# Five stages of a perceiver layer begin with the products of the high rows, and two VectorE steps change places

## The reference

```python
x = x + _L0_xattn_ref(_layernorm(x, axis=-1), mask, ctx, ctx, wq, wk, wv, wo)
x = x + _L0_attn_ref(_layernorm(x, axis=-1), Wqa, g_qa, Wqb, Wkva, g_kva, Wkvb, Wo)
x = x + _L0_ffn_ref(_layernorm(x, axis=-1), router_w, router_bias, w_gate, w_up, w_down, sw_gate, sw_up, sw_down)

# in _L0_xattn_ref: q = x @ wq.T, k_new = x @ wk.T, v_new = x @ wv.T, softmax attention, out @ wo.T
# in _L0_attn_ref:
q_c = rms_norm(hidden_states @ Wqa, g_qa)
q = (q_c @ Wqb)                                  # 16 heads of 128 + 64, the 64 turned (rope)
kv = hidden_states @ Wkva
kv_exp = rms_norm(kv[..., :128], g_kva) @ Wkvb   # keys and values of the heads
# in _L0_ffn_ref: silu(x @ gate) * (x @ up) @ down for each expert, weighted by the router
```

## Time and profile before

| | |
|---|---|
| median of 3 runs | 521.59 us (520.97 to 521.95) |
| the profiled execution | 520.81 us |
| its span, first to last instruction | 519.0 us |
| PE busy | 509.2 us, 98% |
| DVE busy | 402.4 us, 78% |
| ACT busy | 301.6 us, 58% |
| POOL busy | 29.6 us, 6% |
| read from memory | 85.46 MB |

### The profile page before, as it was taken

One profiled execution on the slowest core, in us unless ns is written; L12 is line 12 of the kernel. 1 busy time (PEld: TensorE's weight loads), 2 busy tenths in 40 slices (PEclk: granted clock), 3 DMA queues, 4 the chain that ended last, 5 costly groups with the idle time before them and its releaser, 6 DMA issues.

```text
span 519.0 us, 10261 instructions
## 1 busy us (share of the span) xinstructions
PE 509.2 (98%) x3796; PEld 472.7 (91%) x3796; DVE 402.4 (78%) x627; ACT 301.6 (58%) x437; POOL 29.6 (6%) x49
## 2 busy tenths in 40 slices
PE   9999999999999999989999999999999999999997
PEld 7999999999778998869899999999999999999997
DVE  6776668997888888877797768677776777778675
ACT  5656556873367676665664564646555465655631
POOL 1000000000623113001000000000000000000000
DMA  8765553674412233424536565564646556565521
GB/s 285 302 206 190 170 164 94 191 202 138 152 37 78 77 125 118 130 114 156 211 122 218 159 229 169 197 194 170 228 154 225 174 189 207 165 231 157 210 71 40
DMA packets 19460, 86.25 MB, mean 166 GB/s; under 512 B 2160, under 2 KB 2416, under 8 KB 19312
## 3 DMA queue, kind: packets, MB, share of 16 engines
q1 hardware_dynamic: 19440, 85.99, 49.6%
HBM read 85.46 MB, written 0.52 MB: 166 GB/s over the span
## 4 chain that ended last, share of the span: by engine, by line
PE 81%; DVE 10%; ACT 3%; DMA 3%; issue 2%; SPq 1%; DVEq 0%; ACTq 0%
PE bank L1014 32%; PE bank L443 11%; PE bank L447 11%; PE bank L446 11%; PE bank L451 4%; PE bank L454 4%; PE bank L455 4%; DVE w_lo L296 3%; DMA raw<-ctx_t_dram 1%; DMA raw<-wk_dram 1%; ACT w_hi L291 1%; DVE score_rows L1418 1%; DVE operands L1423 1%; PE bank L792 1%; DVE operands L323 1%
## 5 line engine op out<-in xcount | busy, mean ns | idle before, releaser
L291 ACT CAST w_hi<-raw 128x768 fp32r<-128x768 f32 (+3 forms) x158 | 159.4, 1039 | 95.6 <-PE bank L1014 82.2
L296 DVE TENSOR_TENSOR w_lo<-raw,w_hi 128x1280 fp32r<-128x1280 f32 (+3 forms) x156 | 183.2, 1211 | 14.9 <-ACT w_hi L291 13.9
L1014 PE MATMUL bank<-xt_hi,w_hi 128*128 128x256 f32 x512 | 105.5, 277 | 0.2 <-DVE w_lo L296 0.2
L1014 PE MATMUL bank<-xt_hi,w_lo 128*128 128x256 f32 x512 | 105.4, 277 | 0.0
L1014 PE MATMUL bank<-xt_lo,w_hi 128*128 128x256 f32 x512 | 105.2, 277 | 0.0
L1014 PEld LDWEIGHTS bank<-xt_hi,w_hi 128*128 128x128 f32 x512 | 81.7, 188 | 3.3 <-DVE w_lo L296 0.6
L1014 PEld LDWEIGHTS bank<-xt_lo,w_hi 128*128 128x128 f32 x512 | 79.8, 188 | 0.0
L1014 PEld LDWEIGHTS bank<-xt_hi,w_lo 128*128 128x128 f32 x512 | 79.7, 188 | 0.0
L443 PE MATMUL bank<-w_hi,operands 128*128 128x512 f32 (+1 forms) x194 | 74.9, 386 | 1.0 <-DVE operands L344 1.0
L447 PE MATMUL bank<-w_hi,operands 128*128 128x512 f32 (+1 forms) x194 | 74.1, 382 | 0.0
L446 PE MATMUL bank<-w_lo,operands 128*128 128x512 f32 (+1 forms) x194 | 73.8, 380 | 0.0
(11 more groups left out here) (202 smaller groups left out, 865.4 us busy)
## 6 DMA issues: line engine op xcount, KB each, us to landing
raw<-w_exp_dram SPq DMA_DIRECT2D x34, 896.0 KB, 4.8
raw<-w_exp_dram SPq DMA_DIRECT2D x34, 640.0 KB, 5.6
raw<-ctx_t_dram SPq DMA_DIRECT2D x16, 512.0 KB, 4.4
raw<-ctx_n_dram SPq DMA_DIRECT2D x16, 512.0 KB, 4.0
raw<-w_mla_dram SPq DMA_DIRECT2D x8, 512.0 KB, 3.5
raw<-w_mla_dram SPq DMA_DIRECT2D x8, 448.0 KB, 3.7
raw<-wq_dram SPq DMA_DIRECT2D x4, 256.0 KB, 5.4
raw<-wk_dram SPq DMA_DIRECT2D x2, 512.0 KB, 7.2
```

The lines of the kernel that those rows point to most:

```text
L291: act.copy(w_hi[:, t.slot, at:at + n], raw[:, t.slot, at:at + n]).then_inc(hi_split[k], 1)
L296: eng.tensor_tensor(w_lo[:, t.slot, at:at + n], raw[:, t.slot, at:at + n], w_hi[:, t.slot, at:at + n].bitcast(F32), ALU.subtract) \
L1014: return pe.matmul(bank[b + u][:, m * T:m * T + T], a[:, t.slot, at + m * P:at + m * P + P], x[:, c, :], start=c == 0 and a is w_hi and x ...
```

## The change

At five places a wait for the low part moves behind the products that need only the high part.

- `project_q`: for the first chunk, the products of both weight parts with `xt_hi` come first, for all four column blocks, behind a wait on `ev_hi`; then the four with `xt_lo`, behind the wait on `ev_lo`. Two of the three products of zeros behind the second half's transposes are gone.
- `qkv_half`: a new function `token_rows` does the eight products with `xt_hi` of a half, then what stood `midway`, then the four with `xt_lo`.
- `rope_queries`: two products with `qc_hi`, then the wait, then the one with `qc_lo`.
- The first pair's keys: four products with `kvc_hi`, then the wait, then two with `kvc_lo`.
- `expert_rows` with `split`: the gate's products of each half by `token_rows`.

On DVE, `center(1)` moves ahead of the low parts of half 0. The arithmetic is the same but for the order of the sums in a bank.

```diff
@@ project_q
-                        pe.wait_ge(ev_lo, V_LN1 + 1 + c)
+                        pe.wait_ge(ev_hi if c == 0 else ev_lo, V_LN1 + 1 + c)
+                    if c == 0:
+                        for a, x in ((w_hi, xt_hi), (w_lo, xt_hi), (w_hi, xt_lo)):
+                            if x is xt_lo:
+                                pe.wait_ge(ev_lo, V_LN1 + 1)
+                            for m in range(NC):
+                                pe.matmul(bank[2 + m // 2][:, (m % 2) * T:(m % 2) * T + T],
+                                          a[:, 0, m * P:m * P + P], x[:, 0, :], start=False, stop=False)
+                        continue
...
-                for _ in range(1 + 2 * h):
-                    zeros(7, True)
+                zeros(7, True)
@@ qkv_half
+            def token_rows(o, h, moving, number, told=None, midway=None, first_half=None):
+
+                for c in range(NC):
+                    if c % 2 == 0:
+                        pe.wait_ge(ev_hi, number + c // 2)
+                    hi, lo = moving(c)
+                    ins = pe.matmul(o, xt_hi[:, c, half(h)], hi, start=c == 0, stop=False)
+                    if told is not None and c == 0:
+                        ins.then_inc(told, 1)
+                    pe.matmul(o, xt_hi[:, c, half(h)], lo, start=False, stop=False)
+                if midway is not None:
+                    midway()
+                for c in range(NC):
+                    if c % 2 == 0:
+                        pe.wait_ge(ev_lo, number + c // 2)
+                    ins = pe.matmul(o, xt_lo[:, c, half(h)], moving(c)[0], start=False, stop=c == NC - 1)
+                    if first_half is not None and c == 1:
+                        ins.then_inc(first_half, 1)
+                return ins
+
             def qkv_half(h, midway):
...
-                for c in range(NC):
-                    if c % 2 == 0:
-                        pe.wait_ge(ev_lo, V_LN2 + 2 * h + c // 2)
...
-                    if c == 2 - h:
-                        midway()
+                ins = token_rows(bank[2 + h][:, 0:384], h, columns, V_LN2 + 2 * h, midway=midway,
+                                 first_half=used[0] if h == 1 else None)
@@ rope_queries
-                product(bank[turned(h, g)][:, :], (qc_hi[:, 0, half(h)], qc_lo[:, 0, half(h)]),
-                        (rope_w[:, 0, g, :], rope_w[:, 1, g, :]), True, False, told)
+                pe.wait_ge(ev_hi, V_C + h)
+                ins = pe.matmul(bank[turned(h, g)][:, :], qc_hi[:, 0, half(h)], rope_w[:, 0, g, :],
+                                start=True, stop=False)
...
+                pe.matmul(bank[turned(h, g)][:, :], qc_hi[:, 0, half(h)], rope_w[:, 1, g, :], start=False, stop=False)
+                pe.wait_ge(ev_lo, V_C + h)
+                pe.matmul(bank[turned(h, g)][:, :], qc_lo[:, 0, half(h)], rope_w[:, 0, g, :], start=False, stop=False)
...
-            pe.wait_ge(ev_lo, V_C)
...
-            pe.wait_ge(ev_lo, V_C + 1)
@@ first pair of heads
+            pe.wait_ge(ev_hi, V_C + 3)
+            for hd in range(2):
+                for a in (w_hi, w_lo):
+                    pe.matmul(qk(hd)[:, T:2 * T], a[:, t.slot, 384 + hd * P:512 + hd * P], kvc_hi,
+                              start=False, stop=False, skip_group_check=True)
             pe.wait_ge(ev_lo, V_C + 3)
             for hd in range(2):
-                keys(t, hd)
+                pe.matmul(qk(hd)[:, T:2 * T], w_hi[:, t.slot, 384 + hd * P:512 + hd * P], kvc_lo,
+                          start=False, stop=True, skip_group_check=True).then_inc(bank_full[4 + 3 * hd], 1)
@@ expert_rows
+                    if u == 0 and split is not None:
+                        if h == 0:
+                            ready(t, 0)
+                        ins = token_rows(bank[b][:, 0:I], h, lambda c: wcols(t, c * I, I), split, told=told)
+                        continue
@@ VectorE
             add_attended(1)
+            center(1)
             tokens_lo(dve, 0, V_LN2, xt_hi, xt_lo, 0)
-            center(1)
             tokens_lo(dve, 4, V_LN2 + 2, xt_hi, xt_lo, 1)
```

More of the change, by code:

```diff
@@ L714, in transpose_kv, with columns @@
                 ins.then_inc(bank_full[5 + h], 1)
+            def token_rows(o, h, moving, number, told=None, midway=None, first_half=None):
[16 more added lines that the diff above has]
+                return ins
             def qkv_half(h, midway):
                 t = Tile(0, T_QKV)
-                for c in range(NC):
-                    if c % 2 == 0:
-                        pe.wait_ge(ev_lo, V_LN2 + 2 * h + c // 2)
[L721 to L726, removed]
-                    if c == 2 - h:
-                        midway()
+                def columns(c):
+                    return wcols(t, OFF[c // 2] + (c % 2) * 384, 384)
+                if h == 0:
+                    for k in range(2):
+                        ready(t, k)
+                ins = token_rows(bank[2 + h][:, 0:384], h, columns, V_LN2 + 2 * h, midway=midway,
+                                 first_half=used[0] if h == 1 else None)
                 ins.then_inc(bank_full[2 + h], 1)
@@ L738, in rope_queries @@
             def rope_queries(h, g, told=None):
-                product(bank[turned(h, g)][:, :], (qc_hi[:, 0, half(h)], qc_lo[:, 0, half(h)]),
-                        (rope_w[:, 0, g, :], rope_w[:, 1, g, :]), True, False, told)
+                pe.wait_ge(ev_hi, V_C + h)
+                ins = pe.matmul(bank[turned(h, g)][:, :], qc_hi[:, 0, half(h)], rope_w[:, 0, g, :],
+                                start=True, stop=False)
+                if told is not None:
+                    ins.then_inc(told, 1)
+                pe.matmul(bank[turned(h, g)][:, :], qc_hi[:, 0, half(h)], rope_w[:, 1, g, :], start=False, stop=False)
+                pe.wait_ge(ev_lo, V_C + h)
+                pe.matmul(bank[turned(h, g)][:, :], qc_lo[:, 0, half(h)], rope_w[:, 0, g, :], start=False, stop=False)
             def rope_queries_rest(g):
@@ L981, in expert_rows @@
                             ready(t, k)
-                        if split is not None and u == 0 and c % 2 == 0:
-                            pe.wait_ge(ev_lo, split + c // 2)
                         at = (u * NC + c) * I if k == 0 else OFF[2] + (c - 1) * I
```

## The result

The changed kernel took 518.43 us in the median of 18 executions (517.85 to 525.62), the kernel before 521.27 us in the median of 18 beside it (519.81 to 527.21): a ratio of 0.9944, 95% interval 0.9921 to 0.9966. The gain is 2.84 us where 1.65 us was forecast, and the time lies under the whole range of 518.9 to 520.9.

A forecast was written before the change was run, and what follows sets the result against it. TensorE's work plus its holes bound the kernel, so only holes could be won: 0.4 + 1.25 + 0 = 1.65 us off the profiled 520.81 gives 519.15, plus 0.78 to the median gives 519.9 us; range 518.9 to 520.9.

The forecast's parts named there:

- Place 1: First projection: first product at 8.33 instead of 8.78, shift 0.45 us, of which 0.4 us was taken behind 28.05.
- Place 2: Joint projection with the moved centring: half 1 starts at 136.1 instead of 136.77, a shift of 0.67 us.
- The 0.13 us for a scaling held by GpSimd: Joint projection: the scaling ending half 1's centring waits for GpSimd's weight split; bounds nothing and 0.13 us, 0.13 taken.
- Place 3: Last query products: the stall of some 0.41 us for a low part goes, bringing the shift to 1.1 us.
- Place 4: Key products: wait ends 0.46 us earlier, some 0.15 passes on as TensorE then waits for turned queries; shift 1.25.
- Place 5: First experts: half 0's gain becomes a longer wait for the second expert's weights, about 0.6 instead of 0.3; worth 0.
- Sum: Whole kernel: start 0.4, joint projection through key products 1.25, first experts 0, together 1.65 us.
- signs of being wrong: Half 1's scaling held far longer than 0.13 us, start products spaced by 0.2 us, or the stretch to 158 keeping its end.
- the stretch to 158 us: From the turned queries' transposes at 146.95 to 158: everything hangs on them and moves by the same 1.25 us.
- a shift gained earlier passes through such a stage whole: Long stages with TensorE always busy (29 to 132, 158 to 222 us): nothing to win, earlier shifts pass unchanged.
- the base: Starting time for the forecast: the shown median of 521.59 us, 0.78 above the profiled execution of 520.81.

The follow-up runs named there:

- e3: The kernel before, unchanged, run again as a second draw: 520.31 us beside 520.41 (ratio 1.0013).
- e6: The changed kernel, but VectorE centres half 1 behind the low parts of half 0, as before: 519.66 us beside 521.00 of before (ratio 0.9963).
- e8: The kernel before with zero products ahead of the score loop's six groups, two of 512 columns or one of 128 in turn: 522.48 us in one execution.
- e7: The changed kernel with the key products as before, all behind the wait for the low part: 518.03 us in one execution.
- e1: The kernel before with only the start changed (project_q's high products first, two zero products gone): 520.59 us beside 520.41 of before (ratio 1.0005).
- e12: The same kernel as e1, run again later beside other runs: 521.26 us beside 521.12 of before.
- e2: The changed kernel with the start of the kernel before (project_q order and zero products as before): 518.74 us beside 520.41 of before (ratio 0.9978).

## Why the prediction was wrong

Its moved starts came as it said, and their sum was right to some 0.2 us. Its time was wrong.

- **Place 1.** First product 8.38 (forecast 8.33), wait near 28 us ended at 27.66 (27.65). Over all profiles the first product starts at 8.33 to 8.68 in the ten with place 1 and at 8.76 to 9.22 in the eight without, 0.39 apart in the mean. In the eight profiles whose first projections ran at 118 ns throughout, before and changed, the wait near 28 us ends 19.27 to 19.29 behind that start, so the shift passes whole; in the three at 113 to 114 ns (e3, e6, e8) it ends 18.87 to 18.89 behind it.
- **Place 2.** 0.82 at half 1 (1.18 less 0.36) for 0.67. The 0.13 us for a scaling held by GpSimd was not paid: the row at 132.54 shows its usual 0.49 us, and so do those of the seven other profiles with the move (0.48 to 0.49). The Trainium skill's rule ("SBUF — State Buffer", section "Who interferes with whom"), by which one side stands still, is not borne out at this place; the overlap is only some 0.1 us, and spans on GpSimd are rough. It is borne out 13 us later, where the scaling at 145.95 took 0.75 us in place of 0.17.
- **Place 3.** 1.32 for 1.1, of which 0.15 is what place 2 gave more.
- **Place 4.** The wait moved to the turned queries as forecast, and e7 shows 0.10 to 0.16 passing on, for 0.15. Behind 147 us the shift is 1.47 (1.83 less 0.36) for 1.25, by what places 2 and 3 gave more.
- **Place 5.** Worth 0, by a wait of 0.65 (forecast about 0.6).
- **Sum.** 1.65 forecast. The terms as measured, 0.39 in the mean and 1.47, make 1.86. At the end it is 1.97 and 2.01 between the two pairs of profiles that share a pace in the score stage (0.3 of the 1.97 is the pace of a later stretch), 1.67, 1.88 and 2.1 between means.

None of the prediction's signs of being wrong came: the scaling was not held, the first products were 0.12 to 0.14 us apart (the first four start at 8.38, the next at 8.93, 9.40 and 9.87), and the stretch to 158 us moved.

The step that failed is that "There the granted clock is 1.00 and there is nothing to win; a shift gained earlier passes through such a stage whole". It took the 0.12 us of a product as fixed. The stage had 1.5 us in it: the profile of before shows the slower pace, that of the changed kernel the faster. The kernel alone doesn't settle which (before at 113 ns in e3, the start of the changed kernel at 118 in e6), so that part of the gain between the two profiles is luck. Two later stretches drew the other way and took back 0.2 us (near 97 us) and 0.3 (near 240). So of the 2.7 us between the two profiles some 1.0 is pace, and 1.7 is the change's.

With it failed the base: "The median shown, 521.59, is 0.78 above that execution, so I forecast 519.9 us". A kernel with such clusters has no one time. Over 128 executions before has a mean of 520.59, 1.0 us under the median of the three runs shown. That 1.0, the gain of 1.88 for 1.65, and a median 0.28 under its own mean make up the miss of 1.47 us (1.51 by these figures; this is arithmetic and shows no cause by itself). That the spread of before comes from the paces too is likely, since its two profiles, 1.5 us apart, differ by them; it is not shown for its other executions. The range was made of holes alone and had no room for 1.5 us of pace.

Open: what in the first products of a stretch decides, and whether the earlier start shifts the odds. Of the profiles without a break in the stage, three of the six with place 1 showed 113 ns (the changed kernel twice, e7) and three 118 (e1, e6, e12), and of the three without it two showed 113 (e2, e3): too few to tell. Open too is why three of 17 times with the break stay above both clusters. No version beat the changed kernel: two zero products cost some 0.43 us, about what the settled pace returns on average.

## What to carry to other kernels

Before a small gain is reckoned, count the products in a fixed window of each long stretch in two profiles of the *same* kernel: where the counts differ at full clock, the spread of that pace belongs into the range. Compare means or clusters, and shifts between profiles at equal pace, where medians of two clusters mislead. Of several waits one after the other, only what the last of them loses is won: place 4 closed a wait of 0.58 us and passed on 0.10 of it.

## What the runs showed of the hardware

Back-to-back products of 256 columns, each with its own weights, run at 113 or 118 ns from start to start with the granted clock at 1.00, and keep that pace over 300 products. The pace was the same each time behind the same kind of break in or ahead of the score stage's loop: 113 ns nine times of nine behind two zero products of 512 columns, 118 ns six of six behind one of 512 and four of four behind one of 128. Behind a wait it differed from one execution of a kernel to the next.

A VectorE scaling of 128x2 numbers took 0.75 us where a GpSimd instruction of 0.73 to 0.74 us had begun 0.01 us ahead of it (two profiles), and 0.17 us in the 16 others.
